# Token biases added by GpSimd into dead feature room, and a quad's tanh as one 4096-column ScalarE step

## What is computed

```python
feat = layernorm(x) @ W                      # 4096 rows x 512
txt  = ctx @ Ws                              # 2 x 77 x 512
h    = tanh(txt[:, None, :, :] + feat[:, :, None, :] + b)     # rows x 77 tokens x 512
rho  = einsum('bftd,d->bft', h, w)           # a score for each row and token
att  = softmax(rho + mask)
txt_h = att @ ctx
w_s, b_s = tanh(txt_h @ Wcw.T + bcw), tanh(txt_h @ Wcb.T + bcb)
x = x + w_s * layernorm(x) + b_s
gate = fp4_linear(layernorm(x), w_gate); up = fp4_linear(layernorm(x), w_up)   # 512 -> 1408
x = x + fp4_linear(silu(gate) * up, w_down)  # 1408 -> 512
```

## Time and profile before

| | |
|---|---|
| median of the runs | 1617.54 us |
| the profiled execution's own time | 1617.37 us |
| its span, first to last instruction | 1615.6 us |
| mean granted TensorE clock | 0.983 of full speed |
| TensorE matmul busy | 1449.3 us (90%) |
| ScalarE busy | 1400.3 us (87%) |
| VectorE busy | 1026.1 us (64%) |
| GpSimd busy | 246.4 us (15%) |
| share of the chain that ended last | ScalarE 56%, TensorE 35%, VectorE 8% |

### The profile page before, as it was taken

The page is one execution under the profiler, slowest core; times in us unless marked ns, Lnnn a source line. Parts: engine busy times, 40 slices in busy tenths (PEclk is TensorE's granted clock), DMA queues, the critical chain, the costliest instruction groups (busy, mean ns, idle before and its releaser), DMA issues.

```text
span 1615.6 us, 24215 instructions
## 1 busy us (share of the span) xinstructions
PE 1449.3 (90%) x9752; PEld 637.3 (39%) x9752; DVE 1026.1 (64%) x1703; ACT 1400.3 (87%) x1439; POOL 246.4 (15%) x406
## 2 busy tenths in 40 slices
PE   6988888856898889898999999989999999879997
PEld 3344444412333333343343333433333333445554
DVE  6599998755555425366755454547545555898885
ACT  5999999999999999999999999999999999123331
POOL 1122222200111101011111111101111111022211
PEclk9999999989999999999999999999999999989999
DMA  4133333330110111210221111112111112123332
GB/s 138 41 85 85 79 79 71 90 62 7 25 32 14 38 35 29 38 38 14 42 45 28 38 39 38 38 26 47 43 33 31 38 39 38 38 51 76 75 69 56
DMA packets 180789, 77.91 MB, mean 48 GB/s; under 512 B 163883, under 2 KB 163883, under 8 KB 180677
## 3 DMA queue, kind: packets, MB, share of 16 engines
q1 hardware_dynamic: 179984, 75.00, 20.7%
q10 hardware_dynamic: 693, 1.36, 0.2%
HBM read 27.85 MB, written 8.39 MB: 22 GB/s over the span
## 4 chain that ended last, share of the span: by engine, by line
ACT 56%; PE 35%; DVE 8%; DMA 1%; issue 1%; POOL 0%; SPq 0%; DVEq 0%; POOLq 0%
ACT hring L543 53%; PE rho L698 11%; PE dn L787 6%; PE gu1g L775 2%; PE gu1u L775 2%; PE gu0g L775 2%; PE gu0u L775 2%; ACT sg L563 2%; PE gu0u L725 1%; PE gu1u L725 1%; PE gu1g L725 1%; PE gu0g L725 1%; PE dn L819 1%; DVE stage L1078 1%; DVE garg L1079 1%
## 5 line engine op out<-in xcount | busy, mean ns | idle before, releaser
L543 ACT ACTIVATE hring<-featT,bias 128x1024 f32<-128x1024 f32 x1224 | 1287.4, 1167 | 16.8 <-PE rho L698 16.1
L698 PE MATMUL rho<-hring,wslide 128*32 128x512 f32 x4928 | 603.0, 611 | 125.1 <-ACT hring L543 125.1
L698 PEld LDWEIGHTS rho<-hring,wslide 128*32 128x32 f32 x4928 | 132.3, 110 | 480.9 <-ACT hring L543 265.7
L787 PE MATMUL dn<-wd_room,turned 128*128 128x512 f16 x1023 | 233.3, 380 | 0.0
L1131 DVE TENSOR_TENSOR work<-sg,gu1u 128x352 f32<-128x352 f32 x64 | 33.4, 522 | 274.9 <-ACT sg L563 274.8
L450 POOL TENSOR_SCALAR split_t<-sm 128x88 f32<-128x88 f32 (+2 forms) x91 | 22.4, 246 | 1215.2 <-DVE sm L867 1215.1
L787 PEld LDWEIGHTS dn<-wd_room,turned 128*128 128x128 f16 x1023 | 95.0, 98 | 155.7 <-issue 51.1
L775 PE MATMUL gu0g<-wg,turned 128*128 128x352 f16 x768 | 127.3, 316 | 13.9 <-DMA turned<-xq 10.7
L1131 DVE TENSOR_TENSOR work<-sg,gu0u 128x352 f32<-128x352 f32 x64 | 33.4, 521 | 154.9 <-ACT sg L563 153.8
L775 PE MATMUL gu1g<-wg,turned 128*128 128x352 f16 x768 | 125.5, 313 | 0.0
L775 PE MATMUL gu0u<-wu,turned 128*128 128x352 f16 x768 | 125.4, 313 | 0.0
(11 more groups left out here) (168 smaller groups left out, 1216.0 us busy)
## 6 DMA issues: line engine op xcount, KB each, us to landing
xt<-in_x SPq DMA_DIRECT2D x32, 256.0 KB, 2.9
out<-xt SPq DMA_DIRECT2D x32, 256.0 KB, 2.4
work<-in_x SPq DMA_DIRECT2D x10, 512.0 KB, 3.7
xt<-in_x SPq DMA_DIRECT2D x6, 512.0 KB, 3.8
xt<-in_L_ffn_w_gate SPq DMA_DIRECT2D x11, 256.0 KB, 2.7
xt<-in_L_ffn_w_up SPq DMA_DIRECT2D x11, 256.0 KB, 2.7
work<-in_L_ffn_w_down SPq DMA_DIRECT2D x2, 704.0 KB, 4.3
xt<-in_L_ffn_w_down SPq DMA_DIRECT2D x2, 704.0 KB, 4.1
```

The lines of the kernel that those rows point to most:

```text
L543: act.activation(hring[:, s // 2, g, (s % 2) * 512:(s % 2) * 512 + rows], featT[:, e, ROW0[k]:ROW0[k] + rows], ACT.Tanh, bias=bias[:, e, b ...
L698: last = pe.matmul(rho[SLOTW * g:SLOTW * g + SLOTW, hf * 512:hf * 512 + 512], wslide[:, e, SLOTW - 1 - r:2 * SLOTW - 1 - r], hring[:, s // ...
L787: last = pe.matmul(dn[:, :], hqT[:, a, c, :], wd[:, bb, c, :], start=(c == 0 and i == 0), stop=(c == NC - 1 and i == 2))
```

## The change

For 67 of the 308 quads (in block 1 every fourth from q = 12, in blocks 2 and 3 every third from q = 2) GpSimd adds the token bias to the features beforehand: four `tensor_scalar` adds of 1024 columns, one for each of the quad's tokens, written to the columns of a feature block that is done with (`room_of`, one room for block 1, two for block 2, three for block 3, taken in turn). ScalarE makes such a quad by one tanh step of 4096 columns without a bias column, which waits for the four adds by the new semaphore `summed`. It counts `tanh_ready` up by 4, so TensorE's part is as before. An add waits until the quad that last read its room has been made.

`sum_quads(at)` stands at three places in GpSimd's tile: ahead of `split(D)`, between the two splits, and behind `split(INNER)`. It takes all quads up to `at + AHEAD` that are not yet summed, with `at` = `before[t, 0]`, `before[t, 2]`, `before[t, 4]`.

```diff
+GAP = {1: 4, 2: 3, 3: 3}
+AHEAD = {1: 4, 2: 5, 3: 5}
...
+    summed_quads, room_of, room_from = [], {}, {}
+    last_in = {r: QPB * (r + 1) - 1 for r in range(NBLK)}
+    for k in range(1, NBLK):
+        for q in range(12 if k == 1 else GAP[k] - 1, QPB, GAP[k]):
+            m = QPB * k + q
+            room = len(summed_quads) % k
+            room_of[m], room_from[m] = room, last_in[room]
+            last_in[room] = m
+            summed_quads.append(m)
+    SUMMED = {m: i for i, m in enumerate(summed_quads)}
...
+            def sum_quads(at):
+                while sums[0] < len(summed_quads):
+                    n = summed_quads[sums[0]]
+                    k, q = n // QPB, n % QPB
+                    if n > at + AHEAD[k]:
+                        break
+                    pool.wait_ge(tanh_ready, GRP * (room_from[n] + 1))
+                    to = ROW0[room_of[n]]
+                    for g in range(GRP):
+                        r, e = quad_at(q) if q < QPB - 1 else (FULLR, g)
+                        tok = BATCH_OF[k] * TOK + GRP * r + (g if q < QPB - 1 else 0)
+                        pool.tensor_scalar(featT[:, g, to:to + BLOCKS[k]], featT[:, e, ROW0[k]:ROW0[k] + BLOCKS[k]],
+                                          bias[:, e, tok:tok + 1], None, ALU.add).then_inc(summed, 1)
+                    sums[0] += 1
...
             for t in range(NT):
                 if t + 1 < NT:
+                    sum_quads(before[t, 0])
                     split(D)
+                    sum_quads(before[t, 2])
                     split(INNER)
+                    sum_quads(before[t, 4])
...
+                if n in SUMMED:
+                    act.wait_ge(summed, GRP * (SUMMED[n] + 1))
+                    r = ROW0[room_of[n]]
+                    act.activation(hring[:, s // 2, :, 0:rows], featT[:, :, r:r + rows], ACT.Tanh).then_inc(tanh_ready, GRP)
+                    return
                 for g in range(GRP):
```

More of the change, by code:

```diff
@@ L261, in bass_xattn_fp4_ffn @@
         quad_used = sem("quad_used")
+        summed = sem("summed")
         rho_drained = sem("rho_drained")
@@ L463, in normalise_pair @@
                 pool.wait_ge(pair_normal, 2 * p + 2)
+            sums = [0]
+            def sum_quads(at):
[12 more added lines that the diff above has]
+                    sums[0] += 1
             normalise_pair(0)
```

## The result

| | before | after |
|---|---|---|
| median of the runs beside each other | 1618.99 us | 1904.09 us (1902.45 to 1905.46) |
| ratio | | 1.1761, 95% interval 1.1737 to 1.1786 |
| profiled execution, its span | 1617.37, 1615.6 us | 1904.32, 1902.5 us |
| mean granted TensorE clock | 0.983 | 0.914 |

The kernel is 285 us slower. The prediction had the sign, but 1739 us and a range up to 1800; 165 us of the slowdown were not foreseen.

What follows compares the result with a forecast made beforehand. ScalarE was taken to bound the stage from 403 to 1372 us, busy 965 of 969 us. 1617.4 us plus 163.6 of late sums minus 42.2 saved gave 1738.8, say 1739 us; range 1645 to 1800.

Steps and rivals of the forecast that it cites:

- What an add costs: GpSimd's 1024-column add takes 1.2 us (1.06 to 1.38, at most 1.54), so 4.8 us for a quad's four.
- the prediction's distances: In every tile GpSimd comes free 5.5 us after silu_gate(t, 1) begins and 7.04 us after silu_gate(t, 3).
- The saving: ScalarE's 4096-column tanh step takes 3.53 us instead of 4.16: 0.63 us a quad, 42.2 us for 67 quads.
- The holds: GpSimd's adds and VectorE's steps alternate, adding 2.2 us to a sum between the splits, 5.0 behind the second.
- When GpSimd is free and ScalarE comes: Sums start after GpSimd's splits, too late for ScalarE: 68.9 us late between splits, 94.7 behind the second.
- The cover of the adds: The adds' own 322 us are hidden on GpSimd, idle 845 of 969 us; otherwise the splits would be late.
- VectorE's own delay falls into its waits: VectorE's delay by adds, up to 4 x 1.2 us a sum, is absorbed waiting for sigmoid steps.
- Rival 1: GpSimd and VectorE do not hold each other for long; sums of 4.8 us everywhere, 1649 us; 18% chance.
- Rival 2: Adds get through only when VectorE stops; sums of 7.6 and 11.8 us or more, 1780 to 1825 us; 15%.
- Rival 3: Adds are ready when ScalarE asks, so the 42.2 us come whole: 1575 us; 4% chance.
- Rival 4: TensorE, with 64 us slack, takes over and caps the gain at some 20 us, only under Rival 3; within its 4%.

Runs made afterwards that it cites:

- experiment 4: The changed kernel with a second operation (times 1.0) in each GpSimd add: 1728.91 us, ratio 1.0683 against the kernel before.
- experiment 2: The changed kernel without GpSimd's adds and the wait for them, ScalarE's 67 long steps kept: 1592.95 us, ratio 0.9844 against the kernel before.
- experiment 5: The changed kernel with two-operation adds, quads 165, 168, 242 and 245 left in four steps: 1701.02 us, ratio 1.0512 against the kernel before.
- experiment 3: The changed kernel's one-operation adds made but unused, ScalarE making all quads in four steps without waiting for them: 1682.99 us, ratio 1.0395 against the kernel before.
- experiment 8: Two-operation adds made at the change's places but unused, ScalarE making all quads in four steps without waiting: 1629.25 us, ratio 1.0068 against the kernel before.
- experiment 6: The changed kernel with two-operation adds, each sum made once its room is free: 1629.54 us; with every sixth quad of block 1 instead of every fourth: 1612.26 us.
- 9: The second kernel of experiment 6 with sums bounded by AHEAD 6, 7, 9 and six quads near tiles 8 and 16 in four steps: 1608.96 us.
- 10: Early two-operation sums with every sixth quad in block 1, every fourth in blocks 2 and 3, five left plain, 44 summed: 1604.75 us, ratio 0.9914.

## Why the prediction was right and where it failed

**The step that failed is "What an add costs".** It took 1.2 us between 1.06 and 1.38, at most 1.54, from a 512-column row of 0.771 us with two operations. The add has one, and in that form it takes 2.84 us. The bounds were drawn by size alone; the form was noted in the text and given no price, and no plain `tensor_scalar` in the trace before had one operation. The lower and the upper end were both too low. Four adds are 6.6 us longer than forecast, the holds shorter, and so a sum takes 11.7 us between the splits and 13.0 behind the second, where 7.0 and 9.8 stood. Nearly every late sum stands in ScalarE's order, so the waiting grew by 302.1 - 163.6 = 138 us.

Done again with these sums (12.5 for quads 165 and 242), the count gives some 280 of the 302 us. The rest is what the prediction put at nothing: a second split that a sum makes late, and with it the next sum. In tile 7 this split starts at 875.03, right behind the adds. In tiles 7, 9, 10, 15, 17 and 18 it ends 3 to 5 us later than the prediction's distances say, which gives 22 us more at the six quads behind it. One second sum of a stretch (quad 156) is late too, by 2.5 us. VectorE itself hardly waits for these splits (1.7 us in all).

With the add at its forecast price the time comes out near: experiment 4 runs in 1728.9 where 1739 stood, and with adds of 1.11 us in the prediction's own sum 1729 would stand. That this fits so well is in part luck: the waits for adds are 129 us and not 154, and that is all but made up by 12 us more of waits for TensorE, 6 us of other idle time ahead of the long steps and 3 us less saved. Point by point:

- *The saving.* 0.63 us a quad was forecast; the pace of 3.52 us makes it 0.64, and ScalarE's busy time fell by 39.5 us, 42.2 being forecast. Right. That it would all come through was not: alone it brings 25 us (experiment 2). TensorE's idle time, 64 us over the whole stage, is not spread evenly: it was busy 90% up to 720 us and 95% from there on.
- *The holds.* 2.2 us between the splits and 5.0 behind the second were forecast, 1.1 and 4.0 measured. With adds of 1.11 us and the forecast holds the count makes 154 us of waiting, 129.4 were measured: each hold was a microsecond too large.
- *When GpSimd is free and ScalarE comes.* Right. The longest wait of experiment 4 is 14.7 us (15.95 forecast); that of the change is 21.6, 8.95 and one sum of 12.5. Leaving the four quads of tiles 7 and 15 plain takes 2 x 16 us from those tiles (experiment 5).
- *The cover of the adds.* "If that cover went, the splits would be late": with 12 us a sum it went. Where ScalarE does not wait for the sums that costs 64 us (experiment 3); in the changed kernel it shows as the 22 us above.
- *VectorE's own delay falls into its waits.* Wrong by 11 us (experiment 8), most of it behind the ends of blocks.
- *Rival 1, no holds.* Fallen: adds of 1.11 us have a mean of 1.61 with VectorE beside them, and GpSimd's adds and VectorE's steps go in turn (experiment 6).
- *Rival 2, adds only when VectorE stops.* Fallen by the same timelines; its time came nearer than the forecast's by chance.
- *Rival 3, ready in time.* Not in this order of GpSimd's work; with sums made early it nearly comes about (experiments 6, 9, 10), but the best of them brings 13 to 14 us. Its 44 quads save 26.2 us of busy time, and idle time ahead of the tanh steps, above all for TensorE, takes 13.4 back.
- *Rival 4, TensorE.* Its cap of some 20 us was near: 25. ScalarE's waits for TensorE grew in the changed kernel too (30.5 us in place of 16.8), where the prediction saw only more slack.

The prediction set beside its own sum what the GPSIMD Engine Reference of the Trainium skill (section 3.1) makes of it: 1.03 cycles an element for a body of one or two operations, 1.07 us an add and some 1725 us. For two operations the runs agree, 1.11 us an add and 1728.9, with the luck named above. For one operation they do not: 2.5 ns a column where two take 0.83.

What stays open: why the one-operation form is slower, which no run here looks into; whether a second operation other than a multiplication helps as much; what the 11 us of experiment 8 are made of, one by one; and whether VectorE, in its waits, would make these adds better than GpSimd. That was not tried.

## What to carry to other kernels

Price an instruction from a row of the same form, with as many operations and operands, and not only of the same size; where there is none, run the form a few times behind the kernel's end before building on it. Work put in between the handshakes of an in-order engine should start when its room comes free and not when its result is near, and it must leave the handshakes in time: the same 268 two-operation adds, with ScalarE's saving counted in, cost the kernel 110 us when asked for late and 11 when asked for early. And look at how busy the next engine is, stretch by stretch: here TensorE, 95% busy in blocks 2 and 3, let through about half of what ScalarE saved there.

## What the runs showed of the hardware

- GpSimd's `tensor_scalar` in fp32 takes 2.77 to 2.90 us for 1024 columns with one operation, 1.04 to 1.19 when a multiplication follows, be it by 1.0 or by a column; a copy takes 1.04, a `tensor_tensor` with a broadcast column 1.89.
- GpSimd and VectorE hold each other up in long steps too: adds of 1.11 us take up to 2.49, and a VectorE step of 1408 columns 2.42 in place of 1.62. The hold on VectorE is 0.8 us for an add of 2.97 us as for one of 1.11 (experiment 6), and VectorE's two-input steps run on inside the longer one.
- The granted TensorE clock between 403 and 1372 us was 1.00 before, 0.95 in experiment 4 and 0.89 after the change. At tile 7 of the changed kernel it is seen falling, first in windows (columns as above), then on TensorE:

```profile
853.00:862.00 9.00, 5.18 (x36) 1.60 (x28) 7.45 (x28) 0.53 (x2) 1.58 (x4) 0.92 0.01 2
862.00:875.00 13.00, 0.00 (x0) 0.00 (x0) 12.59 (x13) 0.00 (x0) 12.90 (x5) 0.50 0.17 40
875.00:880.00 5.00, 1.16 (x8) 0.40 (x12) 4.17 (x4) 4.83 (x3) 4.66 (x6) 0.50 0.00 2
880.00:892.00 12.00, 12.00 (x67) 3.26 (x60) 3.15 (x3) 7.10 (x7) 12.00 (x5) 0.82 0.06 11
```

```profile
878.84 3.64 PE L736 MATMUL rho<-hring,wslide 128*32 128x512 f32 x16 [20.66 <-ACT hring L576]
882.41 3.74 PE L825 MATMUL dn<-wd_room,turned 128*128 128x512 f16 x12
886.08 1.92 PE L736 MATMUL rho<-hring,wslide 128*32 128x512 f32 x16
```

  TensorE stands still for 20.66 us in which ScalarE waits for the adds, the grant goes to 0.50 (1.2 GHz), and the first sixteen score matmuls take 3.64 us where the next sixteen take 1.92. So a stall of this length costs some 1.7 us of TensorE on these sixteen. Over the whole kernel the 4928 score matmuls are busy 651.7 us, against 603.0 before. ScalarE's wait for TensorE (30.5 us after, 16.1 before) may hold part of it; how much was not separated.
